# Eight result buffers instead of four in a mixture-of-experts stage with indirect adding transfers

## The chip, the cores and the metric

The kernel runs on one core of a Trainium2 chip. The metric is the device time of one execution in microseconds, given as the median of several runs. One further execution was taken with the hardware profiler; all rows below come from it.

The engines are named as the profile names them: PE is TensorE (PEld its weight loads), DVE is VectorE, ACT is ScalarE, POOL is GpSimd, and SP is SyncE, which computes nothing and only issues transfers and handles semaphores. "SPq" in a row is an instruction of SP's sequencer.

## What is computed

The reference is one layer of a small language model on 8 x 512 tokens with 256 channels: an embedding lookup with a depthwise convolution, an attention without a score matrix, and a mixture of eight experts. Only the last part matters here:

```python
logits = xf @ router_w.T
topw, sel = jax.lax.top_k(sigmoid(logits), 2)          # two experts for each token
topw = topw / (topw.sum(-1, keepdims=True) + 1e-20)
h = jnp.square(jax.nn.relu(jnp.einsum('td,edw->tew', xf, W1e)))   # widths 256 (4 experts), 512 (4 experts)
y = jnp.einsum('tew,ewd->ted', h, W2e)
out = jnp.einsum('ted,te->td', y, combine)             # added to the residual h
```

## The kernel before

**Up to the experts.** Convolution and attention fill the first 500 us or so. They write the residual into `out`, and they scatter each token twice, once for each of its two experts, as a row of 258 numbers (256 channels, the weight, the token's number) into a queue in HBM, `queue_d`, with one stretch per expert. A small table computed on DVE then says for each tile of 128 rows where it begins (`table.row_of`), which expert it has (packed into `table.word_of`), and whether its expert is another than that of the tile before (`table.apart`: 16 if so, otherwise 0).

**The expert stage** (`experts`, from line 1483) works through `TILES` = 71 tiles, the four wide experts (width 512) first, then the four narrow ones (width 256). How many tiles an expert has depends on the data; what is left at the end are filler tiles. Tile j takes this way:

- SP loads its rows into `rows[:, j % 8]` (`load`, L1551). The load of tile j + 8 is issued just before SP allows tile j's addition. It waits until tile j's rows have been used (`row_used`).
- PE turns the rows (`x_turn`, L1693, two steps ahead), multiplies with W1 (`up`, L1703), turns the activations (`act_turn`, L1719) and multiplies with W2 (`down`, also L1703). ACT and DVE split, apply relu and square in between. The result y of tile j comes out in step j + 2.
- ACT copies it from PSUM into `y[:, j % RING]` (`take_y`, L1618). It first waits until the transfer that last read this buffer, that of tile j - RING, has landed.
- DVE copies the tokens' numbers into `token_at[:, j % 8]` (`take_token`, L1653), which waits for the landing of tile j - 8's transfer.
- SP runs `allow(j)` and increments `may_add` (L1563).
- POOL waits for `may_add` and issues the indirect transfer that adds the 128 rows of y onto the rows of `out` which `token_at` names (L1583). When it has landed it increments `added[j % RING]` by 16.

**The order of the additions.** Each token has one row with each of two experts, so within one expert all rows of `out` are different, and additions of one expert may overlap. At a change of expert two tiles can name the same row, so the first tile of an expert has to wait for every addition still under way. SP does this with a value read from the table, without a branch:

```python
def allow(j):
    sp.wait_ge(y_ready, j + 1)
    if j >= RING:
        differs16 = sp.value_load(table.apart[0:1, j:j + 1], min_val=0, max_val=16)
    for before in range(max(0, j - RING + 1), j):
        if before < RING:
            sp.wait_ge(added[before % RING], 16)
        else:
            wait_apart(sp, added[before % RING], differs16 + 16 * (before // RING), sp_passed)
    sp.sem_inc(may_add, 1)
```

`wait_apart` (L139, L140) is one wait on a semaphore against a register's value, whose instruction also increments `sp_passed`. With `differs16` = 16 it waits for the addition of tile `before` itself; with 0 it waits only for the one RING tiles earlier on the same semaphore. For the first tiles, whose `before` is below RING, the wait is for a constant and holds whatever the expert. The sum of the register and 16 * (before // RING) is a separate SP instruction (ALU_OP, L139), made once for each value of before // RING in the loop. Since SP works strictly in order, everything in `allow(j)` stands ahead of the row load of tile j + 9.

Of the kernel before, what the change touches and what calls it, by code (L numbers as in the profile page):

```python
# [78 lines left out]
TABLE = -(-TILES // SLOTS) * SLOTS  # L79
FILLERS = TABLE - TOKENS * TOPK // P  # L80
TURN = 2
RING = 4
TOTAL_W = sum(WIDTHS)


# [1397 lines left out]
def experts(nc, ctx, sem, bank, ident, store, raw_in, table, queue_d, out, w1_parts, w1_lo_ready, w1_zero, queued, stored):  # L1483
    def sbuf(name, shape, dt=F32):
        return ctx.enter_context(nc.sbuf_tensor(name, shape, dt))
# [10 lines left out]
    a_lo = sbuf("a_lo", [P, 2, MAXW], F32R)  # L1496
    y = sbuf("y", [P, RING, DIM])
    token_at = sbuf("token_at", [P, SLOTS], U32)
# [7 lines left out]

    added = [sem(f"added{i}") for i in range(RING)]

    def adds_before(turn, u):

        return turn * (SLOTS // RING) + u // RING

# [26 lines left out]
    def sync(sp):  # L1539
# [13 lines left out]
# [8 lines that stand above are left out]
# [226 lines left out]
```

## Time and profile before

| | us |
|---|---|
| median of 3 runs | 737.45 |
| lowest and highest run | 732.85, 738.35 |
| the profiled execution, its own time | 736.28 |
| its span in the trace | 734.6 |

The span runs from the first to the last instruction of the core; 1.7 us of the execution's time lie around it. The expert stage takes the last third: the first addition is issued 520.75 us after the start of the span, the last at 726.66. The wide experts have tiles 0 to 35, the narrow ones tiles 36 to 68, and tiles 69 and 70 are fillers.

### The profile page before, as it was taken

To read this page: it belongs to the slowest core of one execution; us is meant where nothing else is said; L and a number is where in the kernel's file an instruction comes from. 1 tells how busy PE (TensorE), PEld (TensorE's weight loads), DVE (VectorE), ACT (ScalarE), POOL (GpSimd) and SP (SyncE) were. 2 spreads that over 40 slices of the span, in tenths; PEclk is the share of its full clock that TensorE was granted. 3 is DMA by queue.
4 is the path that set the end of the run, shared out by engine and by line. 5 is a ranking of instruction groups with operands and counts; after the bars stand their busy time and mean duration, and the time that the engine had idled before them with its cause. 6 is when DMAs were issued, how large, how long until landed. Compare 5 with 4: busy or idle time off the path is not lost.

```text
span 734.6 us, 15772 instructions
## 1 busy us (share of the span) xinstructions
PE 632.1 (86%) x5032; PEld 547.8 (75%) x5032; DVE 469.7 (64%) x1216; ACT 306.8 (42%) x668; POOL 322.0 (44%) x292
## 2 busy tenths in 40 slices
PE   6997579999999999999999997523999999988881
PEld 6897457787877878778778785512899999987871
DVE  6475585777779777797787963573554554555540
ACT  3460135343353443533435335330544544555541
POOL 6350250330814608237073260635254454466574
PEclk9999689999999999999999999855999999999996
DMA  6551990010111101112010010423355445466663
GB/s 227 191 105 23 207 341 11 2 57 3 58 58 52 66 1 60 57 45 73 2 59 30 31 57 2 143 95 108 52 83 81 75 82 81 76 112 111 106 97 45
DMA packets 37216, 58.12 MB, mean 79 GB/s; under 512 B 5726, under 2 KB 31066, under 8 KB 36506
## 3 DMA queue, kind: packets, MB, share of 16 engines
q1 hardware_dynamic: 22434, 36.14, 16.9%
q0 software_dynamic: 14160, 20.13, 15.3%
q8 instruction: 61, 1.00, 0.6%
q10 hardware_dynamic: 520, 0.51, 0.2%
q14 instruction: 41, 0.34, 0.2%
HBM read 28.30 MB, written 27.42 MB: 76 GB/s over the span
## 4 chain that ended last, share of the span: by engine, by line
PE 65%; DVE 11%; DMA 7%; issue 5%; ACT 5%; POOL 3%; SPq 3%; DVEq 0%; POOLq 0%; ACTq 0%
PE bank L1311 20%; PE bank L1703 16%; PE bank L1383 8%; DMA out<-y,token_at 5%; PE bank L1354 4%; PE bank L1371 2%; PE bank L1719 2%; PE bank L521 2%; PE bank L522 2%; DVE xn L1009 2%; PE bank L542 2%; PE bank L1340 2%; POOL out L1583 2%; ACT k_exps L895 2%; DVE row L1089 1%
## 5 line engine op out<-in xcount | busy, mean ns | idle before, releaser
L1583 POOL DMA_INDIRECT out<-y,token_at x71 | 111.6, 1572 | 109.7 <-SPq L1563 107.6
L839 POOL DMA_INDIRECT queue_d<-row,slot x64 | 68.8, 1075 | 165.8 <-DVE slot L1148 148.7
L1660 DVE SCALAR_TENSOR_TENSOR act_w<-relu,queue_rows 128x512 f32<-128x512 f32 (+1 forms) x71 | 44.6, 629 | 102.5 <-ACT relu L1606 52.3
L1311 PE MATMUL bank<-xt_hi,w_first 128*128 128x512 f32 x256 | 95.1, 417 | 0.9 <-DVE second_half L1026 0.9
L1311 PE MATMUL bank<-w_first,xt_hi 128*128 128x512 f32 x256 | 83.8, 409 | 2.2 <-DVE xt_lo L1016 1.5
L831 POOL TENSOR_TENSOR second_half<-second_half,q_inv 128x512 f32<-128x512 f32 x64 | 64.9, 1041 | 44.0 <-DVE q_inv L1035 43.8
L887 ACT ACTIVATE second_half<-second_half 128x512 f32<-128x512 f32 x64 | 39.6, 632 | 87.9 <-DVE second_half L1026 87.9
L895 ACT ACTIVATE k_exps<-bank,k_negmax 128x512 f32<-128x512 f32 x64 | 44.1, 690 | 75.3 <-DVE k_negmax L1042 75.1
L1703 PE MATMUL bank<-w_hi,a_hi 128*128 x214 | 66.0, 308 | 1.6 <-DVE a_lo L1666 1.1
L1703 PE MATMUL bank<-w_lo,a_hi 128*128 x214 | 59.9, 280 | 0.1
L1606 ACT ACTIVATE relu<-bank 128x512 f32<-128x512 f32 (+1 forms) x71 | 35.4, 498 | 58.7 <-PE bank L1703 57.9
L1703 PE MATMUL bank<-w_hi,a_lo 128*128 x214 | 59.6, 278 | 0.0
L1311 PEld LDWEIGHTS bank<-w_first,xt_hi 128*128 128x128 f32 x256 | 46.9, 192 | 15.6 <-issue 2.7
L1383 PE MATMUL bank<-g,wv_t 128*128 128x256 f32 x256 | 56.7, 380 | 1.2 <-ACT g L877 1.2
L1311 PEld LDWEIGHTS bank<-xt_hi,w_first 128*128 128x128 f32 x256 | 49.2, 192 | 11.3 <-DVE second_half L1026 1.8
L1023 DVE TENSOR_REDUCE q_max<-bank 128x8 f32<-128x512 f32 x64 | 42.1, 657 | 22.6 <-PE bank L1311 22.6
L1383 PEld LDWEIGHTS bank<-g,wv_t 128*128 128x128 f32 x256 | 48.6, 190 | 8.4 <-ACT g L877 1.6
L1042 DVE TENSOR_REDUCE k_negmax<-bank 128x1 f32<-128x512 f32 x64 | 42.8, 680 | 13.4 <-PE bank L1311 13.1
L1311 PE MATMUL bank<-w_first,xt_lo 128*128 128x512 f32 x128 | 50.9, 398 | 0.0
L1311 PE MATMUL bank<-xt_lo,w_first 128*128 128x512 f32 x128 | 50.8, 397 | 0.0
L1703 PE MATMUL bank<-w_first,x_hi 128*128 x142 | 40.1, 364 | 9.7 <-DVE x_lo L1648 6.5
L1693 PE MATMUL bank<-ident,queue_rows 128*128 128x128 f32 x142 | 27.7, 279 | 23.3 <-DMA queue_rows<-queue_d 23.3
(183 smaller groups left out, 1564.3 us busy)
## 6 DMA issues: line engine op xcount, KB each, us to landing
queue_rows<-queue_d SPq DMA_DIRECT2D x71, 129.0 KB, 2.3
store<-in_L_ffn_w SPq DMA_DIRECT2D x4, 1536.0 KB, 9.2
out<-res SPq DMA_DIRECT2D x8, 512.0 KB, 2.9
h_d<-store SPq DMA_DIRECT2D x6, 512.0 KB, 9.0
h_in<-h_d SPq DMA_DIRECT2D x6, 512.0 KB, 4.0
windows<-taps_d SPq DMA_DIRECT2D x4, 512.0 KB, 5.8
wqk<-in_L_attn_w_qkv SPq DMA_DIRECT2D x1, 2048.0 KB, 13.9
out<-y,token_at POOLq DMA_INDIRECT x71, 4.0
```

What stands on the lines that cost most here:

```text
L831: nc.gpsimd.tensor_tensor(v, v, q_inv[:, b.par, u].unsqueeze(2).to_broadcast([P, 8, DH]), ALU.mult).then_inc(q_ready, 1)
L839: pool.indirect_dma_start(out=queue_d, in_=row[:, t, c, :], in_offset=None, out_offset=bass.IndirectOffsetOnAxis(ap=slot[:, TT * c + t:TT ...
L887: nc.scalar.activation(v, v, ACT.Exp, scale=SCALE).then_inc(q_exp_ready, 1)
L895: nc.scalar.activation(k_exps[:, c % 2], qk_bank(10 + c)[:], ACT.Exp, bias=k_negmax[:, c:c + 1], accum_out=k_sum[:, b.par, c:c + 1]).then_ ...
L1023: link(nc.vector.tensor_reduce(q_max[:, u % 2], src, AX, ALU.max), q_chain, b, Q_LINKS, 2 * u + 1 - (u > 0))
L1042: nc.vector.tensor_reduce(k_negmax[:, c:c + 1], qk_bank(10 + c)[:], AX, ALU.max, negate=True).then_inc(k_max_ready, 1)
L1311: last = nc.tensor.matmul(o, a, c, start=(n == 1), stop=(n == 3 * len(pairs)))
L1383: last = nc.tensor.matmul(tail_bank(6)[:, DIM * kk:DIM * kk + DIM], wv_t[:, a, P * kk:P * kk + P], g[:, a], start=(a == 0), stop=(a == PAI ...
L1583: pool.indirect_dma_start(out=out, in_=y[:, j % RING, :], in_offset=None, compute_op=ALU.add, out_offset=bass.IndirectOffsetOnAxis(ap=toke ...
L1606: nc.scalar.activation(relu[:, u % 2, 0:width], bank[2 + u % 2][:, 0:width], ACT.Relu).then_inc(relu_ready, 1)
L1660: nc.vector.scalar_tensor_tensor(out=act_w[:, u % 2, 0:width], in0=relu[:, u % 2, 0:width], scalar=rows[:, u, DIM:DIM + 1], in1=relu[:, u ...
L1703: last = nc.tensor.matmul(o, a, c, start=(n == 1), stop=(n == parts))
```

## The change

The ring of result buffers gets eight places instead of four. It is one constant:

```diff
-RING = 4
+RING = 8
```

What follows from it in the code: `y` takes 8 KB of each partition instead of 4, and there are eight semaphores `added` instead of four. `take_y` of tile j waits for the landing of tile j - 8's addition instead of j - 4's. In `allow(j)` the loop runs over the last seven tiles instead of the last three. The waits for constants now hold for `before` < 8 instead of < 4, and the value of `apart` is read from tile 8 on instead of tile 4. POOL waits for eight semaphores instead of four at the end. The number of row buffers (SLOTS, 8), the row loads, all arithmetic and the transfers themselves stay as they are.

## Rows read from the trace of the kernel before

**Rows 1.** The page: the chain that ended last, by engine.

```profile
PE 65%; DVE 11%; DMA 7%; issue 5%; ACT 5%; POOL 3%; SPq 3%; DVEq 0%; POOLq 0%; ACTq 0%
```

**Rows 2.** Windows by stage: us, busy of PE, PEld, DVE, ACT, POOL; clock, DMA.

```profile
546.00:640.00 94.00, 94.00 (x660) 85.68 (x659) 48.23 (x112) 47.68 (x109) 43.79 (x28) 1.00 0.50 80
640.00:709.00 69.00, 59.13 (x470) 55.08 (x469) 35.38 (x117) 37.68 (x116) 42.00 (x27) 1.00 0.66 108
709.00:735.00 26.00, 9.58 (x70) 8.31 (x69) 4.68 (x16) 5.94 (x18) 14.44 (x9) 0.76 0.47 55
```

**Rows 3.** Timeline of POOL: additions 35, 36, 37, 44, 45, 63, 68, 70.

```profile
641.74 1.55 POOL L1583 DMA_INDIRECT out<-y,token_at  x1 [1.88 <-SPq L1563]
645.95 1.56 POOL L1583 DMA_INDIRECT out<-y,token_at  x1 [2.66 <-SPq L1563]
648.03 1.55 POOL L1583 DMA_INDIRECT out<-y,token_at  x1 [0.53 <-SPq L1563]
...
662.94 1.56 POOL L1583 DMA_INDIRECT out<-y,token_at  x1 [0.47 <-SPq L1563]
667.72 1.55 POOL L1583 DMA_INDIRECT out<-y,token_at  x1 [3.22 <-SPq L1563]
...
710.99 1.66 POOL L1583 DMA_INDIRECT out<-y,token_at  x1 [0.30 <-issue]
...
720.73 1.56 POOL L1583 DMA_INDIRECT out<-y,token_at  x1 [0.30 <-issue]
...
726.66 1.56 POOL L1583 DMA_INDIRECT out<-y,token_at  x1 [0.31 <-issue]
```

**Rows 4.** L1583 in 645.9 to 710.5 us: POOL's idle time before it, time to landing.

```profile
  SPq L1563: 25.4, 27
...
DMA to landing us min/median/max: 3.8/4.2/5.1
```

**Rows 5.** The chain in 655 to 668 us: SP in `allow(42)`; start, us, what.

```profile
658.44 0.03 SPq L139
...
658.51 0.02 SPq L140
...
658.58 0.02 SPq L140
```

**Rows 6.** The chain in 673 to 685 us: SP between `may_add` of tiles 51 and 52.

```profile
682.59 0.27 SPq L1546
...
683.32 0.33 SPq L1551
...
683.71 0.27 SPq L1557
...
684.57 0.27 issue
```

**Rows 7.** Who waited for whom, 640 to 735 us: total, times, longest.

```profile
ACT y L1618 <- DMA out<-y,token_at: 14.4, 12, 2.8
```

**Rows 8.** Timeline of ACT: the copies of y of tiles 38 and 40.

```profile
646.86 0.38 ACT L1618 ACTIVATE y<-bank 128x256 f32<-128x256 f32 x1 [0.21 <-PE bank L1703]
...
651.23 0.39 ACT L1618 ACTIVATE y<-bank 128x256 f32<-128x256 f32 x1 [0.20 <-PE bank L1703]
```

**Rows 9.** Timeline of POOL: additions 0, 3, 4 and 8.

```profile
520.75 1.61 POOL L1583 DMA_INDIRECT out<-y,token_at  x1 [13.84 <-SPq L1563]
...
533.48 1.56 POOL L1583 DMA_INDIRECT out<-y,token_at  x1 [2.77 <-SPq L1563]
539.32 1.70 POOL L1583 DMA_INDIRECT out<-y,token_at  x1 [4.27 <-SPq L1563]
...
548.65 1.56 POOL L1583 DMA_INDIRECT out<-y,token_at  x1 [1.33 <-SPq L1563]
```

**Rows 10.** PE turning tile 17's rows (557 to 563 us); row loads, 546 to 572 us, to landing.

```profile
L1693 PE MATMUL bank<-ident,queue_rows x2: 272/272/272, 562.0 to 562.1; 128*128 128x128 f32 x2
DMA to landing us min/median/max: 2.0/2.4/2.8
```

## The prediction, made before the changed kernel was run

> **What bounds the kernel now.** I read the page first, then busy time by stage, then POOL's timeline with what released each addition, then the chain in short windows, where SP's instructions show singly.
>
> The page's chain gives PE 65% of the span [rows 1], but that is mostly attention and convolution. The ring is used only in the expert stage, and there the bound changes. With wide tiles PE is busy all 94 of 94 us, and POOL 44 [rows 2]; additions 8 to 35 come (641.74 - 548.65) / 27 = 3.45 us apart [rows 3, 9], set by PE. With narrow tiles PE is busy 59 of 69 us at the full granted clock, and in the last stretch 9.6 of 26 [rows 2]: something else sets the pace.
>
> It is the line of additions. From addition 36 on POOL's idle time before an addition ends 27 times in 27 with SP's increment of `may_add`, 25.4 us in all [rows 4]. So POOL waits for SP. Does SP wait for y? PE's own pace with narrow tiles, where its result and no buffer released the copy, is (651.23 - 646.86) / 2 = 2.19 us a tile [rows 8]. The additions come every 2.0 to 2.1 us between changes of expert: 645.95 to 648.03 for tiles 36, 37, and 648.03 to 662.94 for tiles 37 to 44, 2.13 each [rows 3], one of them of 2.6. That is faster than PE delivers, because SP is working off a backlog. The backlog comes from the changes of expert: addition 45 starts 4.78 us after 44, addition 36 4.21 us after 35 [rows 3]. There SP waits for the landing, 3.8 to 5.1 us after the issue [rows 4].
>
> So three things pace the additions from tile 36: SP's own instructions (at tile 52 from 682.59 to 684.57, 1.98 us and 0.04 to the next: the table's row at 682.59, the row load at 683.32, `apart` at 683.71, the waits, `may_add` [rows 6]; about 2.05 on average; 23 intervals: tiles 37 to 62 without the changes 45, 51, 57); a landing at the four changes 36, 45, 51, 57; and from 63, where no row loads are left for SP, POOL's own pace: 710.99 to 720.73 is 1.95 a tile for five, idle only 0.30 "issue" [rows 3]. Then the change to the filler and the last addition, 726.66, after which only landing and the end remain. y is not on this line. The profile's chain names landings in this stretch even where SP's spacing is its usual one (additions 42 to 44 are such a place); I take the spacing as the evidence there.
>
> **The change, part by part.** *More y buffers.* ACT waited for a ring buffer 12 times, 14.4 us in all, from 640 us on [rows 7]. Those waits shrink or go. But what they delay is y of tiles that SP would only reach later. With the waits gone PE runs ahead until the rows stop it: rows of tile j + 8 are loaded by SP at tile j, need 2.4 us to land [rows 10], and are turned in PE's step j + 6. PE can then lead SP by about one tile more than now. The end is set by the last addition, so this is worth 0. If that cover were gone (additions faster than PE) it would be worth up to the rival's sum below.
>
> *Four more waits in each `allow`.* They sit on SP after y_ready. Waits that are already fulfilled still cost SP time: two in a row start at 658.51 and 658.58, 0.07 us apart, and so does an addition of the register and the wait behind it, 658.44 to 658.51 [rows 5]. Behind them on SP stand `may_add` and then the next row load; POOL waits for the first. Tile by tile:
> - 23 intervals paced by SP, four waits each: 23 x 4 x 0.07 = 6.4 us.
> - The register sum is made once if the loop's tiles lie in one round of the ring, otherwise twice. With four places it is once for j % 4 = 0 or 3, with eight for j % 8 = 0 or 7. So j % 8 = 3 or 4 gets one more: 43, 44, 52, 59, 60, 5 x 0.07 = 0.35 us.
> - At the changes of expert nothing: the first six waits are passed while the seventh, for the landing, still lasts; the interval stays 4.2 to 4.8 us. If that landing were quick (under 2.3 us) the waits would show there too; the shortest is 3.8 [rows 4].
> - Addition 35, the last wide one, comes after its y by the path through SP, now longer by four waits and one sum: 0.35 us, and the landing for 36 moves with it.
> - Wide tiles else: SP's 2.05 + 0.28 = 2.33 us lies under PE's 3.45: 0. From 63 on SP's part is only that from `apart` on, 683.71 to 684.57, 0.9 us [rows 6]; with 0.3 more it lies under POOL's 1.55 + 0.30 [rows 3]. Row loads come later by the shift, but PE needs about 12 us from a row's arrival to its y (2.4 to land, four steps of 2.2, the copy), and SP comes back to that tile after 8 x 2.3 = 18.6 us. Hidden.
>
> Sum: 6.4 + 0.35 + 0.35 = 7.1 us.
>
> *The first nine tiles.* Waits for constants now reach to tiles 5 to 8: each of these additions waits for the landing of the one before, though the expert is the same. Now the additions 1 to 4, which do this already, take (539.32 - 520.75) / 4 = 4.64 us each, against PE's 3.45; addition 8 would start at about 539.32 + 4 x 4.64 = 557.9 instead of 548.65 [rows 9]. `may_add` stands 0.3 us before it, and 0.8 us behind that SP issues the row load of tile 17 (682.59 to 683.32 and the gap ahead [rows 6]), landed 2.4 us later: 557.6 + 0.8 + 2.4 = 560.8. PE turns it at 562.0 [rows 10]. Hidden, by 1.2 us. If each takes as long as addition 4 did (533.48 to 539.32, 5.84 us), tile 17's rows come at 565.6 and PE stalls 3.6 us; with the (533.48 - 520.75) / 3 = 4.24 of additions 1 to 3 the margin is 2.8 [rows 9]. The backlog is worked off at 3.45 - 2.33 = 1.1 us a tile, over by about tile 20, also with the changes between. I take 0 and keep +3.6.
>
> *The end.* POOL's four more waits there are nearly all passed before the last landing: 0 to 4 x 0.07 = 0.3, taken as 0.
>
> The profiled execution took 736.28 us and would take 743.4. The median is 737.45, 1.2 above it; on the median the forecast is 737.45 + 7.1 = 744.6 us, +0.96%.
>
> **The rivals.** *The ring was the limit* (faster). For it speak the 14.4 us of ACT's waits in the stage where PE is idle. Worked out: without SP's share POOL's floor from 641.74 is 35 intervals, five of them changes at 4.5 and 30 at 1.86 (1.55 + 0.30, rounded up), in all 78.3 us, ending at 720.0 instead of 726.66: 737.45 - 6.7 = 730.8 us. It decides if additions wait for y. Against it: SP's spacing at tile 52 is all its own instructions, with no pause [rows 6], and 27 of 27 idle times of POOL end with SP [rows 4]. The Trainium skill (Perfetto Trace Analysis, "Optimization Strategy") says that the same gap repeating on the engine that should be saturated can mean too few buffers for the next tile; by that rule this change gains. The waits of ACT look just like it, but here the repeating gap lies upstream of a slower line.
>
> *Waits cheaper than their spacing.* If the added ones cost only their recorded 0.02 us, or fold together, SP gains 23 x 4 x 0.02 = 1.8 us of work: 737.45 + 1.8 = 739.3. Against it: the spacing of two such waits is 0.07 wherever three follow each other [rows 5].
>
> *The start stalls PE.* As worked out above, +3.6 on top: 748.2. It decides if the four serial additions average over 4.9 us. One of four did.
>
> *The clock falls.* PE will be idle for longer between narrow tiles (59 us of work in 76). If the granted clock drops to its lower level in that stretch, as it does after 709 (0.76 mean) [rows 2], a narrow tile takes PE up to twice 2.19 = 4.4 us and PE sets the pace: 27 x (4.4 - 2.3) = 57 us at most. In 640 to 709 it stayed at 1.00 with gaps of over 2 us, so this is unlikely.
>
> **How the numbers follow.** About 1% is what a measurement of this kernel can tell from no change; here it is 7.4 us. The main case has 0.65: its own range is 741.5 to 747, and it lies around the 1% line, 0.34 above, 0.31 below. The start stalls: 0.14 (slower). Cheaper waits: 0.11 (within 1%). The ring was the limit: 0.07 (faster). The clock: 0.03 (slower). That makes slower 0.51, same 0.42, faster 0.07. The range 739.3 to 749 takes in the cheap waits and the stall at the start; it leaves out the faster case, the clock and the tails.
>
> **What would show it.** Right: additions between changes in the narrow stage 2.3 to 2.35 us apart, POOL idle 0.8 before them and ended by SP; the first y to last y of the narrow tiles not shorter; ACT's waits for landings mostly gone, and PE's waits for queue rows in their place; addition 8 at 556 to 560 us with PE still without a gap up to 640; changes still 4.2 to 4.8. Wrong: additions at PE's pace following y directly, SP's spacing 2.05 as before, or a gap of PE near 562 us.

## The result, and the profile after

| | before | after |
|---|---|---|
| median of 10 runs, us | 736.29 | 743.67 |
| lowest and highest | 732.03, 741.94 | 741.97, 746.95 |
| profiled execution, us | 736.28 | 746.87 |
| span in the trace, us | 734.6 | 745.2 |
| ratio after / before, 95% interval | | 1.011 (1.0074 to 1.0145) |

The change makes the kernel slower by 1.1%, 5 to 11 us by the interval. The forecast was 744.6 us, +7.1. The two profiled executions lie 10.6 us apart, more than the medians; 1.5 us of that stand before the first addition (520.75 and 522.28 us), where the two programs do the same.

The page's chain, after, against [rows 1]:

```profile
span 745.2 us, 16002 instructions
PE 62%; DVE 11%; issue 7%; SPq 6%; DMA 5%; ACT 5%; POOL 2%; DVEq 0%; POOLq 0%; ACTq 0%
```

SP's sequencer goes from 3% to 6% of the chain that ended last, and there are 230 instructions more. Busy time by stage (us of the window, then PE, PEld, DVE, ACT, POOL, each with its count; granted clock, DMA share, GB/s), against [rows 2]:

```profile
546.00:641.65 95.65, 95.65 (x671) 87.14 (x670) 48.45 (x112) 48.61 (x111) 46.85 (x30) 1.00 0.52 83
641.65:719.50 77.85, 63.51 (x480) 58.08 (x478) 37.43 (x121) 40.81 (x121) 42.27 (x28) 0.98 0.59 97
719.50:745.20 25.70, 8.21 (x58) 7.00 (x58) 3.42 (x12) 4.92 (x14) 14.08 (x9) 0.74 0.44 51
```

With wide tiles PE is still busy without a gap. The narrow stage has become longer: 78 us where it was 69. POOL's timeline (start, duration, idle time before and what ended it) for additions 35 to 38, 44, 45, 62, 63, 68 and 70, against [rows 3]:

```profile
643.83 1.55 POOL L1583 DMA_INDIRECT out<-y,token_at  x1 [2.18 <-SPq L1563]
648.13 1.57 POOL L1583 DMA_INDIRECT out<-y,token_at  x1 [2.74 <-SPq L1563]
650.48 1.55 POOL L1583 DMA_INDIRECT out<-y,token_at  x1 [0.78 <-SPq L1563]
653.06 1.56 POOL L1583 DMA_INDIRECT out<-y,token_at  x1 [1.03 <-SPq L1563]
...
668.13 1.56 POOL L1583 DMA_INDIRECT out<-y,token_at  x1 [1.08 <-SPq L1563]
672.43 1.55 POOL L1583 DMA_INDIRECT out<-y,token_at  x1 [2.75 <-SPq L1563]
...
719.73 1.56 POOL L1583 DMA_INDIRECT out<-y,token_at  x1 [1.34 <-SPq L1563]
721.59 1.62 POOL L1583 DMA_INDIRECT out<-y,token_at  x1 [0.30 <-issue]
...
730.97 1.56 POOL L1583 DMA_INDIRECT out<-y,token_at  x1 [0.30 <-issue]
...
737.01 1.56 POOL L1583 DMA_INDIRECT out<-y,token_at  x1 [0.30 <-issue]
```

Addition 36 to addition 62 took 63.2 us before (645.95 to 709.13) and takes 71.6 now. The two changes of expert shown did not grow by more than 0.1 us (4.30 where it was 4.21, 4.30 where it was 4.78), and from 62 to the last addition it is 17.3 us, before 17.5. So the time went into the intervals that SP paces. What each stretch gained or lost in the two traces, worked out from their timelines:

| stretch | before | after | difference |
|---|---|---|---|
| up to the first copy of y | 519.55 | 521.08 | +1.53 |
| to the copy of y of tile 35 (wide tiles) | 120.45 | 120.57 | +0.12 |
| from there to addition 35 | 1.73 | 2.18 | +0.45 |
| change of expert at 36 | 4.21 | 4.30 | +0.09 |
| 23 intervals paced by SP, to 62 | 49.33 | 57.93 | +8.60 |
| changes at 45, 51, 57 | 13.86 | 13.66 | -0.20 |
| additions 62 to 70 | 17.53 | 17.28 | -0.25 |
| to the end of the span | 7.94 | 8.19 | +0.25 |
| sum | | | +10.6 |

Of ACT's waits for a landing from 640 us on [rows 7] the same view shows none any more. Its rows on additions and on row loads (total, times, longest) were, in the kernel before:

```profile
POOL out L1583 <- SPq L1563: 29.8, 29, 3.2
...
PEld bank L1693 <- DMA queue_rows<-queue_d: 0.7, 1, 0.7
```

and are now:

```profile
POOL out L1583 <- SPq L1563: 40.5, 31, 3.3
...
PEld bank L1693 <- DMA queue_rows<-queue_d: 8.6, 9, 2.1
```

PE is held up by late rows instead. y is ready longer before its addition than it was (from the start of the copy to the addition 8.9 us at tile 45, before 5.8), and this buys nothing.

### The profile page after: what moved, and what is told of

Same layout as the page of the kernel before. It is cut to its first block, busy times and chain, and to the rows that moved or that the text cites. A ratio compares the mean times of both kernels' runs of the same rounds, so it can differ in the third digit from the quotient of the medians.

```text
span 745.2 us, 16002 instructions
## 1 busy us (share of the span) xinstructions
PE 636.8 (85%) x5032; PEld 550.4 (74%) x5032; DVE 470.0 (63%) x1216; ACT 308.9 (41%) x668; POOL 323.4 (43%) x292
## 3 DMA queue, kind: packets, MB, share of 16 engines
q0 software_dynamic: 14160, 20.13, 15.2%
## 4 chain that ended last, share of the span: by engine, by line
PE 62%; DVE 11%; issue 7%; SPq 6%; DMA 5%; ACT 5%; POOL 2%; DVEq 0%; POOLq 0%; ACTq 0%
PE bank L1311 20%; PE bank L1703 14%; PE bank L1383 8%; PE bank L1354 4%; DMA out<-y,token_at 2%; PE bank L1371 2%; SPq L1546 2%; PE bank L1719 2%; PE bank L521 2%; DVE xn L1009 2%; PE bank L522 2%; PE bank L542 2%; PE bank L1340 2%; ACT k_exps L895 2%; DVE k_negmax L1042 1%
## 5 line engine op out<-in xcount | busy, mean ns | idle before, releaser
L1583 POOL DMA_INDIRECT out<-y,token_at x71 | 112.6, 1586 | 118.0 <-SPq L1563 116.2
L1383 PE MATMUL bank<-g,wv_t 128*128 128x256 f32 x256 | 58.3, 387 | 1.2 <-ACT g L877 1.2
```

The lines of the kernel that those rows point to most:

```text
L1383: last = nc.tensor.matmul(tail_bank(6)[:, DIM * kk:DIM * kk + DIM], wv_t[:, a, P * kk:P * kk + P], g[:, a], start=(a == 0), stop=(a == PAI ...
L1583: pool.indirect_dma_start(out=out, in_=y[:, j % RING, :], in_offset=None, compute_op=ALU.add, out_offset=bass.IndirectOffsetOnAxis(ap=toke ...
```

## The experiments

Each kernel starts from the kernel before or the changed one and was timed against the kernel before on its own chip. The median of the kernel before was 735.39 us in the first group of four and 746.0 to 746.6 on the chips of the later ones; ratios are therefore what to compare. "Intervals" are the times between `may_add` of one tile and the next for tiles 37 to 62 without the changes 45, 51, 57: 23 of them, from the one trace of each kernel (before 2.145 us on average, after 2.519). Ratios come from many runs, sums of intervals from a single one.

### One part alone: eight buffers, SP's order as before

```diff
-RING = 4
+RING = 4
+YRING = 8
-    y = sbuf("y", [P, RING, DIM])
+    y = sbuf("y", [P, YRING, DIM])
...
-                out=out, in_=y[:, j % RING, :], ...
+                out=out, in_=y[:, j % YRING, :], ...
...
+            if j >= RING:
+                sp.wait_ge(added[j % RING], 16 * (j // RING))
             sp.sem_inc(may_add, 1)
...
-            need(act, added[u % RING], adds_before(turn, u) * 16)
-            nc.scalar.activation(y[:, u % RING], ...
+            need(act, added[u % RING], (adds_before(turn, u) - YRING // RING + 1) * 16)
+            nc.scalar.activation(y[:, u % YRING], ...
```

> One part of the change alone: eight result buffers, but SP's order as before (three waits against the register in each tile, four semaphores, so at most four additions under way), plus one wait for a constant that the shared semaphores need. My theory (SP's instructions pace the additions, result buffers are worth nothing): within 2 us of the kernel before, 0 to +1.6 us; additions in the narrow stage still 2.05 to 2.1 us apart; ACT's waits for a landed addition (14.4 us before) nearly gone, and PE waits for queue rows instead. Rival (the ring was the limit): about 6 us faster.

Measured: ratio 1.0008 (0.9983 to 1.0032), no difference. Intervals 2.136 us. In the waits from 640 us on ACT's waits for a landing are gone, and PE's for rows are there. The first additions of the narrow stage (36 to 38) and the last two:

```profile
645.20 1.56 POOL L1586 DMA_INDIRECT out<-y,token_at  x1 [2.68 <-SPq L1566]
647.30 1.55 POOL L1586 DMA_INDIRECT out<-y,token_at  x1 [0.54 <-SPq L1566]
649.37 1.56 POOL L1586 DMA_INDIRECT out<-y,token_at  x1 [0.52 <-SPq L1566]
...
723.55 1.55 POOL L1586 DMA_INDIRECT out<-y,token_at  x1 [2.57 <-SPq L1566]
725.41 1.56 POOL L1586 DMA_INDIRECT out<-y,token_at  x1 [0.30 <-issue]
```

The idle times of 0.5 us ended by SP stand as before [rows 3]. The buffers alone take all 14.4 us of ACT's waits away, and the kernel gets none of it. The rival that the ring was the limit has fallen. The added wait for a constant cost almost nothing either: it stands in the same instruction as the increment of `may_add`, and the way from the read of `apart` to `may_add` grew from 0.637 to 0.646 us on average.

### The other part alone: waits that are always fulfilled

One, four or eight more waits of the same kind in each `allow` from tile 12 on, with four buffers:

```diff
+EXTRA = 4        # 1, 4 or 8
...
             if j >= RING:
                 differs16 = sp.value_load(table.apart[0:1, j:j + 1], min_val=0, max_val=16)
+            for more in range(EXTRA if j >= 3 * RING else 0):
+                wait_apart(sp, added[more % RING], differs16 + 16 * (j // RING - 2), sp_passed)
```

One:

> The kernel before with its four buffers; from tile 12 on SP passes one more wait that is always fulfilled (and one more addition of the register) in each tile. Theory of the passed waits: 0.14 us on each of 23 intervals and on the entry, +3.4 us. Theory of the slow reads (a read of the table by SP that starts 2.05 to 2.3 us after POOL's last issue lasts until about 2.65): such a read starts here at 1.97, so the reads of the row table stay at 0.27 to 0.31 us on average and nothing is added. Rival (slow reads come with the number of SP's instructions): reads a little longer already here.

Four:

> The kernel before with its four buffers; from tile 12 on SP passes four more fulfilled waits (and one more addition of the register) in each tile: the SP side of the change without its buffers. Passed waits alone: 0.35 us on 23 intervals and the entry, +8.4 us. With the slow reads: reads of the row table start about 2.18 us after POOL's issue, last 0.40 us or more on average instead of 0.31, and the sum is +10 to +11 us. Rival (in the changed kernel something else than SP cost the time, such as the first tiles or the end): less than +3 us here.

Eight:

> As with four more passed waits, but eight. Passed waits alone: 0.63 us on 23 intervals and the entry, +15 us. Theory of the slow reads: the read now starts 2.45 us or more after POOL's issue, behind the bad stretch, so reads of the row table are back at 0.27 to 0.31 us on average, shorter than with four, and nothing is added to the +15. Rival (slow reads grow with SP's load): reads as long as with four waits or longer, +17 us or more.

| | ratio, 95% interval | times 735.4, us | intervals, us | sum of 23 against before |
|---|---|---|---|---|
| one | 1.0048 (1.0022 to 1.0075) | +3.5 | 2.273 | +2.9 |
| four | 1.0103 (1.0071 to 1.0135) | +7.6 | 2.552 | +9.4 |
| eight | 1.0207 (1.0174 to 1.0239) | +15.2 | 2.709 | +13.0 |
| the change | 1.011 (1.0074 to 1.0145) | +8.1 | 2.519 | +8.6 |

Four passed waits without any new buffer cost what the whole change costs. One costs 0.13 us of interval with its addition of the register (0.14 expected), eight cost 0.56 (0.63 expected), but four cost 0.41 (0.35 expected). The step from four to eight is 0.16 us where four more waits should be 0.28. Most of what makes four dearer, and half of what makes eight cheaper, is the read of the row table, which stands right behind `may_add`: within the 23 intervals it took 0.053 us longer than before with four and 0.034 us less with eight. SP's reads of the row table in the narrow stage, duration in ns as min/median/max, of before, after, one, four and eight:

```profile
L1546 SPq TENSOR_LOAD <-row_of x26: 261/271/589, 645.7 to 706.8; - x26
```

```profile
L1546 SPq TENSOR_LOAD <-row_of x26: 263/310/562, 647.9 to 716.6; - x26
```

```profile
L1547 SPq TENSOR_LOAD <-row_of x26: 263/273/513, 644.6 to 710.6; - x26
```

```profile
L1547 SPq TENSOR_LOAD <-row_of x26: 265/362/565, 644.7 to 715.3; - x26
```

```profile
L1547 SPq TENSOR_LOAD <-row_of x26: 262/272/410, 649.0 to 723.1; - x26
```

Their means are 0.310, 0.380, 0.308, 0.368 and 0.287 us: long with four more waits and in the changed kernel, short again with eight. The rival that reads grow long with the number of SP's instructions has fallen. The size was forecast too high for four: reads of 0.40 us or more and +10 to +11 us were expected, and 0.368 us and +7.6 us came (+9.4 in the trace's intervals).

The changes of expert add to the traces' totals: those at 45, 51 and 57 took 5.1 to 5.7 us in the trace with one more wait, and those at 36 and 45 took 5.9 with eight, against 4.2 to 4.8 before, since landings there took up to 5.6 us. Whether that is chance or comes with the waits is not shown; the 23 intervals do not contain it.

### The same instructions in another place

```diff
+        ahead = row_at(SLOTS)
         for j in range(TILES):
             if j + SLOTS < TILES:
-                load(j + SLOTS, row_at(j + SLOTS))
+                load(j + SLOTS, ahead)
+            if j + 1 + SLOTS < TILES:
+                ahead = row_at(j + 1 + SLOTS)
             allow(j)
```

on the changed kernel (eight buffers, seven waits).

> The changed kernel with the same instructions on SP in another place: the read of the row table for the next tile stands right behind the row load instead of right behind may_add, so it starts about 0.9 us after POOL's issue instead of 2.1 to 2.3. Theory of the slow reads: all reads are back at 0.27 us (0.38 on average in the changed kernel), the intervals in the narrow stage fall from 2.52 to about 2.35 us (reads 0.11, and the two-step pattern gone), together 2.5 to 4 us faster than the changed kernel, so +3.5 to +5.5 us on the kernel before. Rival (the lengthening comes with the number of SP's instructions or with fetching them): as the changed kernel, +7 to +8 us.

Measured: ratio 1.0036 (1.0017 to 1.0055), about +2.7 us on the kernel before, and so less than the change's 1.011, with intervals that do not touch. The spacing is 2.358 us. The row table's reads:

```profile
L1546 SPq TENSOR_LOAD <-row_of x25: 263/272/276, 654.5 to 717.4; - x25
```

No long one is left, as expected. The reads now start 0.31 us after POOL's issue, not the 0.9 us of the expectation, which is as far from the bad stretch. The gain over the changed kernel is 3.7 us in the traces (23 intervals of 2.358 against 2.519), within the 2.5 to 4 us expected. By the ratios it is about 5.5 us, so the kernel came out at +2.7 us, below the +3.5 to +5.5 expected. In place of the row table's reads, 12 of the 26 reads of `apart`, which start about 0.9 us after POOL's issue here as before, took 0.35 to 0.41 us; this second, smaller lengthening is not explained.

### Reading the table once a tile

If SP paces the narrow stage, taking work off SP must make the kernel faster, which neither buffers nor anything on PE can. DVE writes `differs16` of tile j and the row number of tile j + 8 into one word:

```diff
-        chained(nc.vector.tensor_scalar(table.apart[:], differs, 16.0, None, ALU.mult))
+        chained(nc.vector.memset(start_f[:, 0:SLOTS], 0.0))
+        chained(nc.vector.tensor_copy(expert_at_8[:, 0:TABLE - SLOTS], start_f[:, SLOTS:]))
+        chained(nc.vector.memset(expert_at_8[:, TABLE - SLOTS:], 0.0))
+        chained(nc.vector.tensor_scalar(differs, differs, 16.0, None, ALU.mult))
+        chained(nc.vector.scalar_tensor_tensor(out=table.apart[:], in0=expert_at_8, scalar=32.0, in1=differs,
+                                               op0=ALU.mult, op1=ALU.add))
...
-        def allow(j):
+        def allow(j, word):
...
+            differs16 = word & 16
...
+            word = sp.value_load(table.apart[0:1, j:j + 1], min_val=0, max_val=...)
             if j + SLOTS < TILES:
-                load(j + SLOTS, row_at(j + SLOTS))
-            allow(j)
+                load(j + SLOTS, word >> 5)
+            allow(j, word)
```

With four buffers:

> Four buffers and three waits as before, but SP reads one word of the table per tile instead of two (row number times 32 plus the 0 or 16), and takes it apart with a shift and a mask. SP's part of a narrow tile falls from 2.05 to about 1.65 us, under POOL's 1.86. My theory (SP paces the narrow stage): additions there 1.86 to 2.2 us apart, paced by POOL and PE in turn, last addition 4 to 6.5 us earlier, 729.5 to 732.5. Rival (SP only seems to pace; the landings or PE set the time): within 1.5 us of the kernel before.

With eight buffers and three waits (the buffers as in the first experiment):

> One read per tile as above, and eight result buffers with SP's three waits (four semaphores). If result buffers become worth something once SP is out of the way: 1 to 3 us faster than with one read and four buffers, since ACT's waits for a landing then hold back a PE that sets part of the pace. If they are worth nothing here either: the same within 1 us.

With the change (eight buffers, seven waits):

> The changed kernel (eight buffers, seven waits) with one read per tile. SP's part is 1.65 + 0.3 = 1.95 us, a little over POOL's 1.86. Theory of SP's pace: additions 1.95 to 2.2 us apart, 8 to 10 us faster than the changed kernel, 1 to 3 us slower than one read with three waits, so -2 to -4 us on the kernel before. Rival (seven waits cost something else than SP's time): still above the kernel before.

| | ratio, 95% interval | times 746.0, us | intervals, us |
|---|---|---|---|
| four buffers, three waits | 0.9947 (0.9928 to 0.9966) | -4.0 | 1.879 |
| eight buffers, three waits | 0.9929 (0.9902 to 0.9957) | -5.3 | 1.898 |
| eight buffers, seven waits | 0.9951 (0.9929 to 0.9973) | -3.7 | 2.044 |

All three are faster than both kernels. With four buffers the last addition came 200.9 us after the first, before 205.9, so 5 us earlier (4 to 6.5 expected). The last row is the changed kernel with one read a tile, and 12 us below it by the ratios (8 to 10 expected). POOL's timeline with eight buffers and three waits, from addition 36 on:

```profile
653.82 1.56 POOL L1592 DMA_INDIRECT out<-y,token_at  x1 [3.15 <-SPq L1571]
655.68 1.55 POOL L1592 DMA_INDIRECT out<-y,token_at  x1 [0.31 <-issue]
657.54 1.56 POOL L1592 DMA_INDIRECT out<-y,token_at  x1 [0.30 <-issue]
659.40 1.56 POOL L1592 DMA_INDIRECT out<-y,token_at  x1 [0.30 <-issue]
```

The idle time is now 0.30 us "issue", and the additions come 1.86 us apart: POOL is the pacer, SP no longer. That holds for 19 of the 23 intervals here and 21 with four buffers (idle 0.32 us or less), but for 4 with seven waits, where SP still sets the pace. Whether the buffers gain something in this kernel is open: 0.9947 and 0.9929 have intervals that overlap, and the 1.3 us between them is what was expected of a small gain and also what chance gives. Between three and seven waits there are 0.15 us of interval (1.898 and 2.044), less than the 0.29 of the waits themselves, since POOL's 1.86 hides a part.

### The first tiles alone

```diff
                 if before < RING:
                     sp.wait_ge(added[before % RING], 16)
+                elif j <= 8:
+                    sp.wait_ge(added[before % RING], 16 * (before // RING + 1))
```

> The kernel before with its four buffers, but additions 5 to 8 wait for the landing of the one before, as in the changed kernel: the start of the change alone. My theory (hidden under PE's wide tiles): additions 5 to 8 come 4.2 to 4.9 us apart, PE stays without a gap to 640 us, and the time is that of the kernel before within 1 us. Four buffers make the cover thinner than in the changed kernel: ACT's copy of tile 12 needs addition 8 landed, at about 561 to 562 us, and comes at 560.8, so up to 1.5 us may show. Rival (the late start carries through to the end): +3 us or more.

Measured: ratio 1.0015 (0.9996 to 1.0033), not to be told from no change. Additions 5 to 8 came 4.16 to 4.53 us apart, and with wide tiles PE had no gap:

```profile
546.00:648.00 102.00, 102.00 (x710) 92.70 (x709) 51.71 (x120) 51.23 (x118) 47.40 (x30) 1.00 0.50 81
```

The late start is hidden even with four buffers: by the interval at most 2.5 us can have come through, less than the rival's 3.

## Why the prediction was right, point by point

- **What paces the narrow stage.** SP's instructions between changes of expert: shown from three sides, by waits added (slower), buffers added (no change) and a read taken away (faster, and POOL's 0.30 us "issue" in SP's place). The traces say it directly too: in all 23 intervals y had been copied at least 2.2 us before its `may_add` (after the change 3.9), so SP never waited for y there. One reading was off: SP's part is 2.145 us on average in the trace before, not about 2.05, since some intervals are longer; the additions were therefore expected 2.3 to 2.35 us apart and came at 2.52. The sum was made of differences, so this did not enter it. The landings named by the profile's chain in [rows 1] were no evidence for this stretch: with SP's work changed they fell from 7% to 5% of the chain while the stretch became longer.
- **More buffers are worth nothing here.** Right. The 14.4 us of ACT's waits [rows 7] lay upstream of a slower line. By the Trainium skill (Perfetto Trace Analysis, "Optimization Strategy") the same gap repeating on the engine that should be saturated can mean too few buffers. ACT, which waited here, was busy 37.68 of 69 us [rows 2] and is not that engine, so the prediction stretched the rule where it let this change gain by it; eight buffers alone gained nothing.
- **Four passed waits, 0.07 us each.** Right in place and size. `allow(37)` in the changed kernel passes them one by one, here four of the seven and `may_add` (chain, 649.6 to 650.3 us):

```profile
649.94 0.02 SPq L140
...
650.00 0.02 SPq L140
...
650.07 0.02 SPq L140
...
650.14 0.02 SPq L140
...
650.19 0.02 SPq L1563
650.21 0.04 issue
650.25 0.52 SPq L1546
```

- **The term that was too small.** For the 23 intervals the sum had 6.4 + 0.35 = 6.75 us; the trace shows 8.6. The step that failed is that it took SP's other instructions as unchanged. The last row above is what it left out: the read of the row table, 0.52 us where it usually takes 0.27. Split up, the 8.6 us are 6.5 between the read of `apart` and `may_add`, where the waits and the register sums stand (6.75 forecast), 1.8 in these reads (0.315 to 0.393 us on average in the 23 intervals), and 0.3 for the rest, in the main one more of the pauses described in the last section, four instead of three.
- **Entry at tile 35.** 0.35 forecast, 0.45 measured. With four passed waits and four buffers it grew by only 0.14, so in a single trace this term is little more than scatter.
- **Changes of expert.** Unchanged, as forecast: the passed waits hide under the landing.
- **The first nine tiles.** The price was 0 with a margin of 1.2 us at tile 17's rows. Addition 8 started 36.57 us after addition 0 (558.85 - 522.28), forecast 37.2; PE stayed without a gap. PE turned tile 17's rows at about 563.6 (1.5 us later than before, like everything in this execution); their load was issued at 559.36 and had 4.2 us. The cover held.

These additions, against [rows 9] (0, 3, 4, 8 and 9):

```profile
522.28 1.61 POOL L1583 DMA_INDIRECT out<-y,token_at  x1 [14.39 <-SPq L1563]
...
535.63 1.56 POOL L1583 DMA_INDIRECT out<-y,token_at  x1 [2.66 <-SPq L1563]
540.30 1.56 POOL L1583 DMA_INDIRECT out<-y,token_at  x1 [3.11 <-SPq L1563]
...
558.85 1.56 POOL L1583 DMA_INDIRECT out<-y,token_at  x1 [3.29 <-SPq L1563]
560.94 1.55 POOL L1583 DMA_INDIRECT out<-y,token_at  x1 [0.54 <-SPq L1563]
```

- **The clock.** It was granted in full with wide tiles and at 0.98 on average in the narrow stage (before 1.00). The 0.98 is one drop to the lower level, from 694.4 to 697.8 us, after PE had sat idle for 1.91 us from 691.9 on. So the fourth rival's condition did come true for 3.4 us, and it had a chance of 0.03. It cost nothing that the traces show, since the copies of y began 6.6 us or more before their additions in that stretch; that PE would set the pace did not happen. The prediction's argument against this rival, PE gaps of over 2 us at the full clock in the kernel before, is not in the trace: the longest there between 640 and 709 us is 1.08 us.
- **The size.** +7.1 forecast; +7.4 by the medians, +8.1 by the ratio. With the slow reads the sum is 8.9 us, which the interval of the ratio holds as well. That the missing term was small beside the spread of the runs is luck. The prediction's own line of 1%, between slower and no change, lies inside the interval of 0.74 to 1.45%, so its 0.51 against 0.42 is not decided by the runs.

## What to carry to other kernels

A queue that only waits and issues has a price per instruction even when every wait has long been fulfilled, here 0.07 us; where it paces the kernel, count its instructions like matmuls, let a wait share an instruction with an increment where the order allows it (0.01 us here), and prefer one read of a packed word to two. Before buying buffers for an engine that waits for them, look at what paces the end of the line: the wait that repeats may be upstream of it, and then it only moves (here from ACT's buffers to PE's rows). A loop of fixed instructions can change its length when its phase against another engine's transfers changes, so after an insertion look again at the instructions that stayed.

## What the runs showed of the hardware that was not expected

**SP's reads of a word from SBUF depend on when they start.** All 1170 reads of a table's word with a start between 0.2 and 4.3 us after POOL's last issue of an addition, in the eleven profiled kernels:

| start after the issue, us | reads | mean, us | longer than 0.35 us |
|---|---|---|---|
| 0.2 to 0.8 | 81 | 0.273 | 1 |
| 0.8 to 1.0 | 207 | 0.282 | 21 |
| 1.0 to 1.9 | 307 | 0.264 | 0 |
| 1.9 to 2.0 | 52 | 0.322 | 13 |
| 2.0 to 2.1 | 63 | 0.431 | 41 |
| 2.1 to 2.3 | 97 | 0.448 | 88 |
| 2.3 to 2.4 | 36 | 0.350 | 16 |
| 2.4 to 2.6 | 29 | 0.306 | 5 |
| 2.6 to 4.3 | 298 | 0.268 | 1 |

A read that starts from 2.0 to 2.3 us after the issue usually lasts until about 2.6 us after it. At 2.1 us the addition's first packets appear. The busy share of the 16 DMA engines in the kernel before, 720.73 to 724.73 us, which is addition 68 from its issue on, in 40 slices of 0.1 us:

```profile
DMA  1099977989974421000009932769999630000000
```

The first 16 slices are the addition before; from slice 22 on, 2.1 us after the issue, come this one's own. So the slow reads are under way at about the time when a transfer's first packets appear. It is not the packets as such: 139 reads started 2.6 to 3.3 us after the issue, in the middle of them, and took 0.270 us on average. What makes a read last up to 0.6 us is not shown: no run changed the packets themselves. In the kernel before SP's loop usually put the read at 1.77 to 1.88 us, just ahead of the stretch; four more waits moved most of them to 2.1 to 2.4, into it; eight moved them to about 2.45, behind it. The long reads in the row from 0.8 to 1.0 us are another case, they end at about 1.26 us; they come from two kernels alone, the one with the read in another place (16) and the one with the first tiles alone (5).

**SP pauses after every 128 of its instructions.** Between tiles 8 and 63 each of the eleven traces has a pause of 0.33 to 0.38 us between two of SP's instructions at a distance of exactly 128 recorded instructions, at 72 of 76 such places. Where SP paces the kernel, more instructions therefore cost this as well: the 23 intervals hold three such pauses in the kernel before and four after the change. What SP does in them is not shown.
